# A top-32 search in fifteen pieces of two segments instead of thirteen of three, a query fetch split in two, and a sum over heads by pairs

## The reference, cut to what matters

```python
Q = (x_text @ Wq).reshape(Bb, Tt, H, DH)          # 1024 rows, H = 4 heads, DH = 32
K = (x_vision @ Wk).reshape(Bb, Gg, H, DH)        # 6404 rows
scores = jnp.einsum('bthd,bghd->bhtg', Q, K) / np.sqrt(DH).astype(np.float32)
topv, topi = jax.lax.top_k(scores, K_TOP)         # K_TOP = 32
probs = jax.nn.softmax(topv, axis=-1)
attn = jnp.zeros_like(scores).at[bi, hi, ti, topi].set(probs)
attn_mean = attn.mean(axis=1)                     # over the 4 heads
c_t = jnp.einsum('btg,bgd->btd', attn_mean, V)
```

## Time and profile before

| | |
|---|---|
| median of 3 runs | 1713.12 us (1707.66 to 1718.37) |
| profiled execution, its own time | 1714.1 us |
| its span | 1712.2 us |
| VectorE busy over the span | 1280.9 us (75%) |
| GpSimd busy over the span | 706.9 us (41%) |
| first MAX8 of the search to the last | 618.4 to 1185.0 us |
| first exponential of the weighing to the last | 675.9 to 1245.4 us |

### The profile page before, as it was taken

How to read it: one execution, slowest core, us unless ns; L and a number is a source line. 1 busy time by engine, 2 the same in 40 slices (tenths; PEclk the granted TensorE clock), 3 DMA queues, 4 the chain that set the end, 5 groups by cost and what they waited for, 6 DMA issues and landing times. The chain is left out here.

```text
span 1712.2 us, 20081 instructions
## 1 busy us (share of the span) xinstructions
PE 1399.5 (82%) x6652; PEld 718.6 (42%) x6653; DVE 1280.9 (75%) x3087; ACT 943.4 (55%) x1500; POOL 706.9 (41%) x545
## 2 busy tenths in 40 slices
PE   5777799999987657889888898988957539999798
PEld 2223344333334512455454444544645423333365
DVE  4999667855515669999999999999948566766433
ACT  4665211566623302888888888888821236666321
POOL 2664212022002000989998898989810030000012
PEclk9899899999997967999999999999978658999899
DMA  6000111000009420000000000000030120000000
GB/s 148 1 1 0 33 56 42 0 1 0 0 5 201 86 63 1 1 1 1 1 1 1 1 1 1 1 1 1 1 96 9 34 64 1 1 1 1 1 1 13
DMA packets 29962, 37.34 MB, mean 22 GB/s; under 512 B 12975, under 2 KB 23087, under 8 KB 28723
## 3 DMA queue, kind: packets, MB, share of 16 engines
q1 hardware_dynamic: 27294, 22.31, 4.8%
q10 hardware_dynamic: 2552, 13.63, 3.9%
HBM read 29.68 MB, written 6.24 MB: 21 GB/s over the span
## 5 line engine op out<-in xcount | busy, mean ns | idle before, releaser
L1557 PE MATMUL psum<-film_ka,film_context_qa 97*128 97x512 bf16 (+1 forms) x832 | 323.7, 390 | 89.3 <-DVE search_and_weigh_e L1791 38.1
L1758 DVE MAX8 search_and_weigh_kept<-psum 128x8 f32<-128x171 f32 (+2 forms) x1216 | 331.5, 327 | 14.4 <-PE psum L1559 14.1
L1559 PE MATMUL psum<-film_kb,film_context_qb 128*128 128x512 bf16 (+1 forms) x832 | 320.3, 386 | 0.0
L1944 ACT ACTIVATE search_and_weigh_e<-psum,search_and_weigh_bias 128x512 f32<-128x512 f32 (+1 forms) x416 | 268.1, 666 | 60.6 <-PE psum L1559 58.7
L1791 DVE SCALAR_TENSOR_TENSOR search_and_weigh_e<-psum,film_context_top,search_and_weigh_e 128x512 f32<-128x512 f32 (+1 forms) x283 | 200.6, 716 | 14.2 <-ACT search_and_weigh_e L1944 12.4
L1814 POOL TENSOR_TENSOR search_and_weigh_e<-search_and_weigh_e,search_and_weigh_keep 128x512 f32<-128x512 f32 (+1 forms) x133 | 150.6, 1132 | 100.1 <-ACT search_and_weigh_keep L1923 96.8
L1557 PEld LDWEIGHTS psum<-film_ka,film_context_qa 97*128 97x128 bf16 x832 | 86.0, 103 | 237.9 <-DVE search_and_weigh_e L1791 103.3
L3057 POOL TENSOR_TENSOR residual<-residual,top_expert_kept 128x1024 f32<-128x1024 f32 x7 | 16.4, 2348 | 295.4 <-DVE top_expert_kept L3014 295.4
L1818 POOL TENSOR_TENSOR search_and_weigh_mean<-search_and_weigh_e 128x512 f32<-128x512 f32 (+1 forms) x104 | 133.5, 1284 | 11.5 <-DVE search_and_weigh_e L1791 4.3
L1848 PEld LDWEIGHTS psum<-ctx_rows,search_and_weigh_mean_T 128*128 128x128 f32 (+1 forms) x816 | 122.6, 193 | 30.4 <-issue 4.1
L1823 POOL TENSOR_TENSOR search_and_weigh_mean<-search_and_weigh_mean,search_and_weigh_e 128x512 f32<-128x512 f32 (+1 forms) x104 | 128.0, 1230 | 8.2
(11 more groups left out here) (549 smaller groups left out, 2642.6 us busy)
## 6 DMA issues: line engine op xcount, KB each, us to landing
film_kb<-film_k_rows ACTq DMA_DIRECT2D x4, 1601.0 KB
film_ka<-film_k_rows ACTq DMA_DIRECT2D x3, 1601.0 KB
ctx_T<-in_ctx_T SPq DMA_DIRECT2D x1, 2401.5 KB
gqa_experts_w<-in_L_ffn_W SPq DMA_DIRECT2D x1, 2048.0 KB
film_convolve_back<-in_dft_back SPq DMA_DIRECT2D x1, 1728.0 KB, 13.3
film_k_rows<-cross_attention_film_hi SPq DMA_DIRECT2D x6, 256.0 KB, 2.1
film_k_rows<-cross_attention_film_mid SPq DMA_DIRECT2D x6, 256.0 KB, 2.0
film_k_rows<-cross_attention_film_low SPq DMA_DIRECT2D x6, 256.0 KB, 2.0
```

Source lines behind the costliest of these rows:

```text
L1557: pe.matmul(out, a["qa"][0:ROWS, h, rows], a["ka"][0:ROWS, h, c + b:c + b + cols], start=True, stop=False)
L1559: last = pe.matmul(out, a["qb"][:, h, rows], a["kb"][:, h, c + b:c + b + cols], start=False, stop=True)
L1758: last = dve.max(kept[:, h % 2, first + s, :], bank[:, lo:hi])
L1944: act.activation(e[:, n % RING, sub, 0:PIECES[u][1]], ps[:, SEARCH_BANKS + q % WEIGH_BANKS, 0:PIECES[u][1]], ACT.Exp, bias=bias[:, i % 2, ...
```

## The change

The search of a head is cut into 15 pieces of 427 keys (426 for one in fifteen) in place of 13, each of two segments of 213 or 214 keys, so 30 segments for a head. The walk over slots stays, with a rule (`searched_at`) that gives 11 of every 13 slots one piece and 2 of them two. `pick` works on 240 kept numbers. GpSimd adds two pairs of heads in one instruction of 128x2x512 and then the two sums. The seven fetches of `split_queries` bring only the first tile's 128 columns; seven others, issued by SyncE at the head of the next block, bring the other 896, and TensorE waits for them before it searches tile 1.

```diff
-PIECES = [(c, min(HALF, S2 - c)) for c in range(0, S2, HALF)]
-N_SEG = sum(len(segments(w)) for _, w in PIECES)
+SEARCHES, PER_PIECE = 15, 2
+N_SEG = SEARCHES * PER_PIECE
+SEARCH_EDGES = [round(k * S2 / N_SEG) for k in range(N_SEG + 1)]
...
+def fetch_queries(eng, a, k, cols, done):
+
+    for name, r in QUERY_PLACES[k]:
+        eng.dma_start(a[name][r * DH:(r + 1) * DH, :, cols],
+                      a["q_rows"][k].rearrange("(h d) s -> d h s", d=DH)[:, :, cols]).then_inc(done, 16)
...
-            fetch(0, ((qa, 0), (qb, 0), (qb, 2)))
-            fetch(1, ((qa, 1), (qb, 1), (qb, 3)))
-            fetch(2, ((qa, 2),))
+                fetch_queries(act, a, k, slice(0, P), spread)
...
+    def searched_at(G, sub):
+
+        k = NH * G + sub
+        return range(k * SEARCHES // NCH, (k + 1) * SEARCHES // NCH)
...
+                for r in searched_at(G, sub):
+                    head, after = r // SEARCHES - 1, r % SEARCHES
...
+                        for s, (lo, hi) in enumerate(search_columns(u)[2]):
+                            last = dve.max(kept[:, h % 2, PER_PIECE * u + s, :], bank[:, lo:hi])
+                            if s == 0 and picking:
+                                pick(head, 2 * after)
+                        last.then_inc(searched, 1)
...
             if last_tile(n):
+                if n >= MEANS:
+                    pool.wait_ge(mT_psum, n - MEANS + 1)
+                link(pool.tensor_tensor(out, w[0], w[1], ALU.add))
                 pool.wait_ge(summed_ready, n + 1 - (NT - 1) * NCH)
+                pool.tensor_tensor(out, out, w[2], ALU.add).then_inc(mean_ready, 1)
             else:
-                link(pool.tensor_tensor(w[2], w[2], w[3], ALU.add))
-            pool.tensor_tensor(out, out, w[2], ALU.add).then_inc(mean_ready, 1)
+                pairs = e[:, n % RING, :, 0:width].rearrange("p (a b) k -> p a b k", b=2)
+                link(pool.tensor_tensor(pairs[:, :, 0, :], pairs[:, :, 0, :], pairs[:, :, 1, :], ALU.add))
+                if n >= MEANS:
+                    pool.wait_ge(mT_psum, n - MEANS + 1)
+                pool.tensor_tensor(out, w[0], w[2], ALU.add).then_inc(mean_ready, 1)
...
+                if r == NH * SEARCHES:
+                    pe.wait_ge(a["other_tiles"], 16 * N_FETCHES)
...
+                for r in searched_at(G, sub):
+                    search(r + SEARCH_LEAD)
...
+                for k in range(3):
+                    fetch_queries(sp, a, k, slice(P, S), a["other_tiles"])
```

More of the change, by code:

```diff
@@ L1746, in vector @@
             for sub in range(NH):
-                r = NH * G + sub
-                head, after = r // NCH - 1, r % NCH
-                picking = searching and 0 <= head < NT * NH and after < PICKS // 2
-                if search_piece(r):
-                    i, h, u = search_piece(r)
-                    dve.wait_ge(search_done, r + 1)
-                    if u == 0 and i * NH + h >= 2:
-                        dve.wait_ge(picked, PICKS * (i * NH + h - 1))
-                    first = sum(len(segments(w)) for _, w in PIECES[:u])
-                    bank = ps[:, r % SEARCH_BANKS, :]
-                    for s, (lo, hi) in enumerate(segments(PIECES[u][1])):
-                        last = dve.max(kept[:, h % 2, first + s, :], bank[:, lo:hi])
-                        if s == 0 and picking:
-                            pick(head, 2 * after)
-                    last.then_inc(searched, 1)
-                elif picking:
-                    pick(head, 2 * after)
-                if picking:
-                    pick(head, 2 * after + 1)
+                for r in searched_at(G, sub):
+                    head, after = r // SEARCHES - 1, r % SEARCHES
+                    picking = searching and 0 <= head < NT * NH and after < PICKS // 2
+                    if search_piece(r):
+                        i, h, u = search_piece(r)
+                        dve.wait_ge(search_done, r + 1)
+                        if u == 0 and i * NH + h >= 2:
+                            dve.wait_ge(picked, PICKS * (i * NH + h - 1))
+                        bank = ps[:, r % SEARCH_BANKS, :]
+                        for s, (lo, hi) in enumerate(search_columns(u)[2]):
[3 more added lines that the diff above has]
+                        last.then_inc(searched, 1)
+                    elif picking:
+                        pick(head, 2 * after)
+                    if picking:
+                        pick(head, 2 * after + 1)
                 i = limits_tile(G)
```

34 lines of the change are left out of this document (14 added, 20 removed).

## The result

The changed kernel takes 1703.53 us (median of 8, 1700.25 to 1705.59) where the kernel before took 1714.55 beside it (median of 8). The ratio is 0.9934, with a 95% interval of 0.992 to 0.9948: 11 us faster, where 28 were forecast. Its profiled execution took 1702.9 us, its span is 1701.1. The time lies just inside the forecast range of 1669 to 1704.

A forecast was written before the change was run, and what follows sets the result against it. VectorE was taken to set the pace, with GpSimd, ScalarE and TensorE close behind. Mixed stage 19, search alone 3 and fetch 6 made 28 us off the profiled 1714.1: 1686, median 1685 us, range 1669 to 1704.

The forecast's parts named there:

- Fetch: Query fetch before the search: with the first tile's columns fetched alone, TensorE starts 6.1 us earlier, between 4.5 and 6.5.
- search alone: The first 60 slots, before weighing starts: VectorE's search and picks save 4.4 us, taken as 3 after TensorE's clock.
- The 1.4 us that the clock was to take off search alone: In search alone, TensorE's low granted clock early on was to cut the 4.4 us saving to 3.
- Instructions: Expected durations in the new profile: MAX8 about 0.373 us, picks 0.395, GpSimd's pair additions 2.35.
- The price of a MAX8 by the Trainium skill: VectorE's search: 0.125 us fixed cost per PSUM read, 17 us more saved over 32 heads, giving 1668; chance 0.05.
- the forecast by rows: VectorE's search and picks priced from profile rows: 0.96 us saved a head, 26 us mixed stage, 4.4 search alone.
- The hold: Longer GpSimd additions hold VectorE's three small limit instructions longer in each of seven tiles: 21 x 0.24 = 5 us back.
- The allowance for the neighbours: Mixed stage: step taken 0.18 us above the busiest engine, up from 0.15, giving 5.50 us a step.
- the neighbours take over: Rival: TensorE, ScalarE and double slots hold the mixed step at 5.65 or more; whole 1699 to 1704; chance 0.17.
- The sum of the mixed stage: Search and weighing together: 0.21 us less a step over 89 steps, 19 us saved, ends 26 and 9.
- The pairs: GpSimd's paired addition: 2.43 us for 2.70, 0.27 less a step; rival that they cost more than two additions, chance 0.05.

The follow-up runs named there:

- warm: Changed kernel plus 18 TensorE matmuls of 256 columns, results unread, ahead of the second score of a tile's first step; 1695.58 us, ratio 0.986.
- bias_free: Changed kernel with a tile's bias and limits made by eight one-column VectorE instructions instead of three; 1683.92 us, ratio 0.9817 to the kernel before.
- before_bias_free: Kernel before the change, with only the bias and limits made by eight one-column VectorE instructions; 1708.02 us, ratio 0.9968.
- bias_free_three_adds: bias_free with GpSimd's three additions of 512 columns back in place of the pairs; 1695.95 us, ratio 0.9902 to the kernel before.
- limits_free: Changed kernel with all small operations of a tile's limits written as twelve short VectorE instructions with one tensor input; 1708.37 us, ratio 0.9944.
- warm_norelu: warm without ScalarE's second instruction for a mask (the Relu after the Sign), so the output differs; 1670.23 us, ratio 0.9733.
- bias_free_even: bias_free with the search in 13 equal pieces, one per slot, four of three segments, still 30 segments a head; 1681.54 us, ratio 0.9818.

## Why the prediction missed

**Fetch, search alone: right.** 6 and 3 us forecast, 5.8 and 4.3 in the traces, and 6 for the fetch on its own. The 1.4 us that the clock was to take off search alone are hardly seen.

**Instructions: right.** MAX8 0.373 us (0.373 forecast), picks 0.395 (0.395), pairs 2.357 (2.35). Back to back, the new MAX8 start 0.29 us apart, as counted. The price of a MAX8 by the Trainium skill (VectorE: DVE Perf Modes, "The TRN2 errata"), with 17 us more, isn't seen in busy time: VectorE's is 23 us less over the whole span (1280.9 and 1257.5), and the forecast by rows counted 26 and 4; some 4 us of the difference are the longer holds, which count as busy.

**The hold: right in size by luck, wrong in what hangs on it.** "21 x 0.24 = 5 us back to VectorE" is, in the runs, 1.8 - 1.1 = 0.7 us a tile, 4 us over the mixed stage. But it was priced as a mean over random meetings of three instructions, and none is random: L1796 meets the pair addition 0.27 us after its start in each tile and lasts 2.08 us where it lasted 0.98, L1798 stays at 1.10, and L1788 became shorter (0.96 and 0.48). The first failing step is that the sum stopped there. Behind the held pair stands the mask, behind the mask TensorE, and 2.5 us of idle TensorE brought its clock from 1.00 to 0.50. The prediction looked for the clock only in search alone. In the mixed stage, six falls where there had been one cost 5 x 1.45 = 7 us.

**The allowance for the neighbours: the second failing step.** "With the neighbours nearer I raise that to 0.18." With held limits out of the way, a step is 73.9 / 13 = 5.68 us before and 71.95 / 13 = 5.53 after. VectorE's busy time per step is 5.54 (97.4% of 320, 311.78 us) and 5.24 (94.6%). So the step is 0.15 above the busiest engine before, as the prediction read it, and 0.30 after, where 0.18 was allowed. (The prediction's 5.71 divides 320 us by 56 steps; at 75.0 us a tile there are 55.5, of 5.77.) VectorE and GpSimd got their 0.30 and 0.27 us a step, and half came through: 12 us in the mixed stage where 24 were counted before the hold. The rival "the neighbours take over" had this mechanism, with the step at 5.65 or more as its mark. The measured time falls into its 1699 to 1704, but not by its mechanism alone: the step of 75.2 / 13 = 5.78 has the boundary in it, and cleared of that it is 5.53, between the rival and the forecast.

The sum of the mixed stage is then -12 + 4 + 7 = -1 us, measured -0.6, forecast -24 + 5 = -19. Taken as differences of whole mixed stages (after 508.5, warm 500.3, bias_free 489.5, before 509.1, before_bias_free 501.8) the same terms are -12.2, +3.4 and +8.2. Both signs of the forecast's terms held; one loss was missing and one gain was twice what it could be. Why half of the relief didn't come through is argued from the experiments with less work and not shown.

**The pairs** are neither free nor dear: worth 11 us of span when nothing is held (1693.0 in bias_free_three_adds, 1681.6 in bias_free; ratios 0.9902 and 0.9817), a loss of 7 in the kernel before, and in the changed kernel not told apart from nothing (0.9945 and 0.9934).

## What to carry to other kernels

Look for the tiny instructions that stand at a serial point of the loop, and put beside each what GpSimd does at that moment: here they were held to the end of GpSimd's instruction, at the same place in every tile, and merging two instructions of GpSimd's raised one such hold from 1.0 to 2.1 us (to 1.5 in the kernel before). Count what waits behind them down to TensorE, and ask what the idle time does to its clock; in this kernel that cost more than half of the mixed stage's gain. Where several engines are within a tenth of the pace, relief of one is worth what an experiment with lighter work returns, here three tenths, not its full size.

## What the runs showed of the hardware

A VectorE addition of four columns lasted 0.15 us free and 2.08 us behind an addition of 1024 columns on GpSimd; a TENSOR_SCALAR of four columns with one input lasted 2.32 us in the same way and those of 32 columns, 0.39 in the median of limits_free, up to 2.33, while none of the 64 of one column in bias_free, 56 of which ran during one of GpSimd's, took over 0.216. By the Trainium skill (SBUF — State Buffer, "SBUF: two separate sides") the lock is taken by a VectorE instruction with two SBUF inputs or in a 2-port mode. The one-input holds fit the second case if those instructions ran in that mode, which the trace doesn't show.

TensorE's clock fell after 2.4 to 2.5 us of idle time in one piece, with a piece of 0.7 to 0.9 us shortly ahead, at six boundaries of six, and after pieces of 1.03, 0.71 and 1.44 us at four of six with otherwise equal tiles. In warm_norelu it fell after 2.33 us at one boundary and stayed up after 2.06 to 2.12 us at five; in bias_free_even it stayed up after 1.55 us at six of six. Eighteen matmuls a tile that compute nothing of use brought the changed kernel from 0.9934 to 0.986 of the kernel before: 8 us by the medians (1703.53 and 1695.58), and 8.2 in the mixed stages of the traces.
